# Two of fourteen tiles made one slice earlier, and one read back issued later in the setup

## The reference

```python
X0 = embedded_features                 # (1024, 39, 16)
Xi = X0
for W, b in Ws:                        # three layers, H = 128
    Wr = W.reshape(H, 39, Fi)
    Xi = einsum('hjk,bjd,bkd->bhd', Wr, X0, Xi) + b[None, :, None]
    res.append(Xi.sum(axis=2))
h = concatenate(res + [dense_ctx], axis=1)
h = relu(h @ W_top1 + b_top1); h = relu(h @ W_top2 + b_top2)
y = h @ W_top3
```

## Time and profile before

| | |
|---|---|
| median of three runs | 1356.19 us |
| the profiled execution | 1354.27 us |
| its span, first to last instruction | 1352.5 us |
| PE busy | 1273.0 us, 94% |
| DVE busy | 1061.5 us, 78% |
| ACT busy | 1052.3 us, 78% |
| POOL busy | 957.1 us, 71% |
| mean granted clock of PE | 0.977 |

### The profile page before, as it was taken

The page is one execution under the profiler, slowest core; times in us unless marked ns, Lnnn a source line. Parts: engine busy times, 40 slices in busy tenths (PEclk is TensorE's granted clock), DMA queues, the critical chain, the costliest instruction groups (busy, mean ns, idle before and its releaser), DMA issues.

```text
span 1352.5 us, 20729 instructions
## 1 busy us (share of the span) xinstructions
PE 1273.0 (94%) x6069; PEld 1039.2 (77%) x6069; DVE 1061.5 (78%) x2683; ACT 1052.3 (78%) x3352; POOL 957.1 (71%) x693
## 2 busy tenths in 40 slices
PE   3279999999999999999999999999999999999998
PEld 3257677787878888788877878788887888778877
DVE  4158888978798778977889778977789777987895
ACT  2248888887888878887888878887788878887784
POOL 6778888867887778867888777877788455564201
PEclk7579999999999999999999999999999999999999
DMA  6252412132222412232222322214122221220000
GB/s 227 35 120 60 74 46 70 45 51 55 54 50 57 74 31 54 62 51 55 55 60 46 60 49 51 60 46 74 45 53 49 49 60 50 53 53 15 1 2 0
DMA packets 68522, 74.38 MB, mean 55 GB/s; under 512 B 47363, under 2 KB 52996, under 8 KB 68282
## 3 DMA queue, kind: packets, MB, share of 16 engines
q1 hardware_dynamic: 58426, 70.49, 22.4%
q0 software_dynamic: 9984, 2.58, 2.2%
HBM read 12.64 MB, written 2.56 MB: 11 GB/s over the span
## 4 chain that ended last, share of the span: by engine, by line
PE 80%; DVE 7%; issue 5%; ACT 3%; POOL 2%; SPq 2%; DMA 1%; DVEq 0%; ACTq 0%; POOLq 0%
PE ring L1082 19%; PE ring L1084 18%; PE ring L1083 18%; PE side L969 5%; PE side L1004 4%; PE l_ps L955 4%; PE l_ps L956 3%; PE l_ps L957 3%; DVE x_r L827 3%; DVE terms L871 2%; ACT terms L658 2%; PE side L1033 1%; PE side L1042 1%; SPq L343 1%; POOL e_in L406 1%
## 5 line engine op out<-in xcount | busy, mean ns | idle before, releaser
L658 ACT ACTIVATE terms<-ring,xb 128x128 f32<-128x128 f32 x2944 | 844.2, 404 | 210.1 <-PE ring L1084 197.1
L871 DVE SCALAR_TENSOR_TENSOR terms<-ring,xb,terms 128x128 f32<-128x128 f32 x1792 | 507.8, 344 | 96.7 <-PE ring L1084 94.2
L1082 PE MATMUL ring<-w_hi,x_hi 128*128 128x512 f32 (+1 forms) x1280 | 556.2, 435 | 11.1 <-DVE terms L871 5.9
L1084 PE MATMUL ring<-w_hi,x_lo 128*128 128x512 f32 (+1 forms) x1280 | 497.9, 389 | 0.0
L1083 PE MATMUL ring<-w_lo,x_hi 128*128 128x512 f32 (+1 forms) x1280 | 497.2, 388 | 0.0
L827 DVE TENSOR_REDUCE x_r<-terms 128x32 f32<-128x800 f32 (+1 forms) x512 | 463.5, 927 | 0.1
L450 POOL TENSOR_TENSOR pairs_lo<-pairs,pairs_hi 117x1024 fp32r<-117x1024 f32 (+1 forms) x104 | 250.4, 2408 | 174.9 <-ACT pairs_hi L553 174.4
L406 POOL DMA_INDIRECT e_in<-in_tbl,idx x312 | 306.5, 982 | 76.3 <-issue 69.4
L1082 PEld LDWEIGHTS ring<-w_hi,x_hi 128*128 128x128 f32 x1280 | 241.7, 189 | 74.6 <-DVE terms L871 14.7
L1084 PEld LDWEIGHTS ring<-w_hi,x_lo 128*128 128x128 f32 x1280 | 240.8, 188 | 52.3
L1083 PEld LDWEIGHTS ring<-w_lo,x_hi 128*128 128x128 f32 x1280 | 242.7, 190 | 43.6
(11 more groups left out here) (114 smaller groups left out, 692.7 us busy)
## 6 DMA issues: line engine op xcount, KB each, us to landing
pairs<-x_both SPq DMA_DIRECT2D x303, 156.0 KB
x_rep<-x_both SPq DMA_DIRECT2D x45, 156.0 KB
e_in<-in_tbl,idx POOLq DMA_INDIRECT x312
terms<-in_L_rec_W SPq DMA_DIRECT2D x1, 2496.0 KB, 11.2
x_scratch<-e_df SPq DMA_DIRECT2D x8, 312.0 KB, 9.2
xb<-x_scratch SPq DMA_DIRECT2D x8, 312.0 KB, 5.2
g_t<-in_L_rec_W SPq DMA_DIRECT2D x4, 512.0 KB, 6.0
g_t<-x_both SPq DMA_DIRECT2D x8, 156.0 KB
```

What stands on the lines that cost most here:

```text
L658: last = nc.scalar.activation(term(d, ACT_BEFORE[d][g] + i), twos(ring[:, (GROUPS * d + g) % RING, i * H:(i + 1) * H]), ACT.Copy, scale=sc ...
L871: nc.vector.scalar_tensor_tensor(out=acc, in0=y, scalar=scale_of(j, d, odd), in1=acc, op0=ALU.mult, op1=ALU.add).then_inc(dve_unit, 1)
L1082: nc.tensor.matmul(acc, x1_hi[:, x], w1_hi[:, w], start=True, stop=False)
L1084: nc.tensor.matmul(acc, x1_lo[:, x], w1_hi[:, w], start=False, stop=True).then_inc(y_group, 1)
```

## The change

Tile 0 of the next chunk is made in slice 6 instead of 7, and its tile 7 in slice 14 instead of 15; PE still multiplies them in slices 8 and 0. In these two slices POOL multiplies behind its two gathers and blocks, ahead of the fold, and not at the head of its slice. ACT's `pair_upper` moves with `tile_made`, to group 7 of slices 6 and 14. In the setup the read back of the scales goes behind the loads of tile 5 instead of those of tile 2.

```diff
     FIRST_MADE = 7
+    LATE_MADE = (6, 14)
 
     def tile_made(c, d, layer1, following):
 
-        if d < PAIR_TILES - 1:
-            return (c, PAIR_TILES + 1 + d) if layer1 else None
-        if d == D - 1:
-            return (c + 1, PAIR_TILES) if following else None
-        if not FIRST_MADE <= d < FIRST_MADE + PAIR_TILES:
-            return None
-        return (c + 1, d - FIRST_MADE) if following else None
+        if d < PAIR_TILES - 1 and layer1:
+            return (c, PAIR_TILES + 1 + d)
+        if layer1:
+            made = {6: 0, 14: PAIR_TILES}.get(d, d - FIRST_MADE if FIRST_MADE < d < D - 1 else None)
+        elif d == D - 1:
+            made = PAIR_TILES
+        else:
+            made = d - FIRST_MADE if FIRST_MADE <= d < FIRST_MADE + PAIR_TILES else None
+        return (c + 1, made) if following and made is not None else None
...
                     for i in range(0 if layer1 else FROM_PE, PAIR_TILES):
                         pair_tile(c + 1, i, 1 - odd)
-                        if i == (0 if layer1 else FROM_PE + 1):
+                        if i == (0 if layer1 else PAIR_TILES - 2):
                             xb_back()
...
-                    if made:
+                    if made and d not in LATE_MADE:
                         multiply_pairs(*made)
...
                             make_block(c - 1, r, 1 - odd)
+                    if made and d in LATE_MADE:
+                        multiply_pairs(*made)
                     if layer1 and d in FOLDED:
```

## The result

The changed kernel takes 1356.43 us (median of 20 runs, 1355.79 to 1359.88); the kernel before, run between them, 1354.57 us (20 runs, 1353.23 to 1357.32). The ratio is 1.0015 [1.0008, 1.0022]: 1.9 us slower, inside the 0.2% that I had called no change, though the interval does not reach 1.0000.

What follows compares the result with a forecast made beforehand. PE was taken as the bound (80% of the chain), so other engines count only where PE waits or setup is delayed. Read back -0.85, chunk 0 +2.0, chunks 1 to 6 +0.1, slice 14 0: +1.25, 1357.4 us on the median; range 1354.3 to 1360.2.

Steps and rivals of the forecast that it cites:

- The sum of the prediction: All terms on the whole kernel: -0.85 + 2.0 + 0.1 + 0 = +1.25 us.
- The stall: Chunk 0, slice 6: POOL's late product holds ACT's group 7 and so PE; +2.0 us, bounds +1.5 and +2.5.
- the relief in slice 7: Chunk 0: group 7 of slice 7, without a rounding in front, may save PE a tenth or two.
- Chunks 1 to 6: Slice 6 there: the product mostly fits POOL's idle hole of 1.48 us; 0 to 0.05 us a chunk, 0.1 in all.
- slice 14: Chunks 0 to 6: ACT's group 7 some 0.25 us late, hidden by PE's slack; value 0, bounds -4.7 and +1.8 us.
- longer holds in every chunk: Rival, slice 6 of chunks 1 to 6: later products hold ACT; 0.5 us a chunk adds 3.0, 1360.4 us; chance 0.10.
- relief at the chunk's end: Rival: ACT's lighter slice 15 removes PE's 0.67 us wait at seven chunk ends; 1352.7 us; chance 0.13.
- chunk 0 hides its hold: Rival, slice 6 of chunk 0: POOL starts earlier or PE has slack, so no +2.0 us; 1355.4 us; chance 0.11.
- The clock in chunk 0: Rival: PE's stall drops its clock; 6.83 us at half speed costs 3.4 us, 1360.8 us; chance 0.07.
- The read back: Setup: moving it brings tile 3 some 2 us earlier, of which PE passes on 0.85; -0.85 us, bounds -0.85 and +2.2.
- the read back gains nothing: Rival, setup: the read back gains nothing where it now stands; 1358.3 us; chance 0.11.
- the base: The profiled 1354.27 us, taken as 1.92 us under the median, to which the +1.25 us was added.

Runs made afterwards that it cites:

- Moving ACT's place alone: The changed kernel, but in slice 6 ACT rounds the tile ahead of group 9 instead of group 7: 1355.28 us, ratio 1.0001.
- leaving chunk 0 out: The changed kernel, but chunk 0 makes its tile 0 in slice 7 as before the change: 1354.70 us, ratio 1.0000.
- the extra matmuls: Never-read matmuls in PE's idle setup stretches, added to the kernel before: 1354.97 and 1354.37 us; with the read back also moved: 1353.38 and 1352.80 us.
- twins: Two kernels with the same never-read setup matmuls, read back unmoved against moved: 1354.97 against 1353.38 us, then other matmul counts, 1354.37 against 1352.80 us.
- the kernel with the tiles alone: The changed kernel with the read back of the scales left where it was, only the two tiles moved: 1356.76 us, ratio 1.0018.
- the kernel with the product ahead: The changed kernel with slice 6's product at the head of POOL's slice, ahead of gathers and blocks: 1354.94 us, ratio 1.0003.
- nine matmuls: The changed kernel plus nine never-read matmuls on PE in chunk 0's slice 6, ahead of the second block matmul: 1356.28 us, ratio 1.0012.

## Why the prediction was right or wrong

**The direction, and chunk 0: right.** The sum of the prediction was +1.25 us; measured are +1.9 us. The stall was put at 2.0 us more and is 2.07 us, for the reason given: PE's wait of 2.49 us against "some 2.5", POOL's product and ACT's rounding in the order and with the durations of the sum. Moving ACT's place alone took the loss away, and so did leaving chunk 0 out. The prediction also named the relief in slice 7, at "a tenth or two"; it is some 0.3 us.

**Chunks 1 to 6, slice 14 and the chunk's end: right.** The wait in slice 6 stayed at 0.42 us in each of the six, those for DVE at 0.7 us at most and 5.9 us in all, and everything of the change but chunk 0's tile of slice 6 gave a ratio of 1.0000. The rivals *longer holds in every chunk* and *relief at the chunk's end* fall with that, and *chunk 0 hides its hold* by the 2.49 us.

**The clock in chunk 0: it falls, but for less.** I gave the rival 3.4 us. After a stall of 2.49 us the clock did fall, to 0.57 over the 4 us behind it. The Trainium skill (TensorE: Matmul & The Clock Gate, section "Part 1: The HAM clock gate") says that the throttled state is the default and that recent activity lifts it; the trace agrees with that, by the 0.57. The cost was 0.56 and 1.07 us in two executions. The rival was mis-sized in two ways: the fall of 6.83 us from which I took it was longer, and I counted no wait that would take up slow matmuls.

**The read back: the step that failed.** The prediction had -0.85 us; alone it gave +0.4 us with an interval from -0.8 to +1.6 us (0.0003 [-0.0006, 0.0012] of 1354.6), so a small gain is not quite excluded, but it is less than I had. Two links held: tile 3 came early (74.67, predicted 75.1), and PE took tile 2 behind the turned weights without a wait. The link that failed is that the first turned weights "end at 76.55 + 2.15 = 78.70 and do not depend on it". In the changed kernel PE first stood 1.14 us for tile 1, whose low part DVE makes behind the product of tile 2, now at 71.84 instead of 71.41; and the turned weights ran at the 1.2 GHz level nearly to their end, 3.26 us. ACT's copies of them, behind which tile 3's rounding is queued, began at 80.27 instead of 78.74, and DVE, waiting for that rounding, came to tiles 5 and 6 no earlier than before.

With the extra matmuls the move was worth 1.6 us between twins, twice, and 1.33 us at tile 6 where both twins still had the high clock: more than the 0.85 us that I had called the most. That bound was wrong too, since it took PE's pace from rows at the low clock. No gain of the read back was seen in the kernel as changed, which is what the rival *the read back gains nothing* says; that the clock's level is the cause is argued and not shown. In the kernel that leaves out chunk 0's tile the first turned weights took 2.16 us, and the product of tile 6 still came at 87.34: PE had reached them only at 77.81, 1.26 us later than before, with DVE's product of tile 2 at 72.65. And three executions of the changed kernel had a mean granted clock of 0.997, where sixteen others had 0.975 to 0.977; they took 1355.86, 1356.35 and 1356.90 us, around the median and not under it. Where in them the clock was up is not known. Why the clock came up later, near 80 us and not near 77, is open: the kernel with the tiles alone, whose setup is that of before, came up late as well (0.66 over 75 to 80 us, where before had 0.80), so it is not shown to follow from the read back.

**The absolute time.** 1357.4 us was predicted and 1356.43 measured. The three runs before had a median of 1356.19 us, the twenty 1354.57: the base was 1.6 us too high, the sum 0.6 us too low. That the two partly cancel is luck; the sum is short mainly by the 0.85 us of the read back that did not come.

## What to carry to other kernels

When an operation is moved a slice earlier, look first at the in-order queue of its consumer: what stands behind the new wait there, in the first pass of the loop too, where the engines are in other phases than in the steady state. A hole seen in chunk 3 says nothing of chunk 0; the loss here was one stall in one chunk. And two changes that each gain nothing alone, here the read back's move and the extra matmuls, can gain together: try them together before either is dropped, and compare the clock of the twins stretch by stretch before the gain is put down to one cause.

## What the runs showed of the hardware that was not expected

Extra matmuls in a setup that were never read cost nothing measurable (ratios 1.0001 and 0.9991), and beside them a DMA change that alone showed nothing (1.0003) was worth 1.6 us. The granted clock fell behind one stall of PE of 2.49 us in the changed kernel (0.57 over 168 to 172 us) and of 2.50 us with the tiles alone (0.69); it did not behind one of 1.14 us, in the kernel with the product ahead (1.00 throughout 108 to 176 us), nor where nine matmuls filled the long one (1.00).
